# Blank rows of a sorted-token buffer written in an earlier stage, and one operand of a sum moved to TensorE

## The chip, the cores and the metric

One core of one Trainium2 chip runs the whole program. The metric is the device time of one execution in microseconds (us), the median of several runs. The core has TensorE (PE, with its weight loads as PEld), VectorE (DVE), ScalarE (ACT), GpSimd (POOL) and SyncE (SP), each with its own list of instructions; semaphores hold them together. The 16 DMA engines move data between HBM and the on-chip memory (SBUF).

## The reference

The input is x of 4 x 1024 tokens with 128 channels, float32. Four layers follow one another, each closed by a layer norm of x plus what the layer computes. Cut to what matters:

```python
x = _layernorm(x + _L0_attn_ref(x, ...))   # attention over channels' heads: 32 heads of 1024 keys of 64
x = _layernorm(x + _L0_ffn_ref(x, ...))    # attention with 16 heads, then 8 experts, top 2
x = _layernorm(x + _L1_attn_ref(x, ...))   # convolution, a scan over time, a gate
x = _layernorm(x + _L1_ffn_ref(x, ...))    # 8 experts; of a token's top 2 the one with the higher number counts
```

In the third layer, with `out_ssm` the scan's output through two products and their biases:

```python
x_res = jax.nn.silu(out_ssm @ W2.T)
z = out_ssm * x_res
return out_ssm + z @ Wlast.T
```

so the next norm takes x + out_ssm + z @ Wlast.T. In the fourth layer each token goes through one expert only.

## The kernel before, in words

The stages follow one another with a barrier between them. A tensor of tokens lies in SBUF with channels on the 128 partitions and the 4096 tokens along a partition (`xT` and `y`, in turn input and output of a stage).

**First attention** (`first_attention_stage`, from 23 to 493 us of the span). 32 heads; a head has 8 groups of 128 keys. Per group TensorE makes scores in PSUM (L315), VectorE takes the negated maximum (L388), ScalarE the exponential (L376), GpSimd scales the values (L423), TensorE mixes (L325). Beside groups 0 and 2 TensorE projects the next head's keys and queries (L294, L301), and ScalarE copies them out behind groups 2 and 4. The keys are needed on both halves of the partitions: SyncE doubles them by two DMAs per head (`double`, L274), which wait for the copied keys; the scores of the next head wait for the doubled keys. Behind each of the first 13 doublings SyncE issues one load of constants for the next stage (`loads`, L282). From the 14th head on it does nothing but double. Before the first product TensorE waits for two memsets of VectorE (L391, L392).

**Merged stage** (`scan_stage`, from 1441 to 1570.6 us), the scan. Blocks k = 0 to 15 are (batch, half of 512 tokens, group of 128 hidden channels), four to a batch. TensorE makes raw steps (L1617) and inputs (L1623); ScalarE four functions, the positive part, a square and the decay; GpSimd two products per block (`ratio`, L1749 and L1755); VectorE five operations per block (`step_size`), ending in `delta` and `b_bar`. At the end of a batch VectorE runs two scans of 1024 elements (L1805). Then, two batches of turns later in each engine's hand-written order: TensorE's `outs` (L1631, L1634), ScalarE's `take_out` into `out` (L1712), TensorE's `residuals` (L1643), ScalarE's silu into `res` (L1721), VectorE's `gate` (L1813), TensorE's `lasts` (L1653), and VectorE's `finish` (L1819). In parallel GpSimd adds the stage's input x to `out` (`add_x`, L1762) into `x_out`, and `finish` adds `x_out` and the product of `lasts` into y. `outs` of the next batch's second half waits for `finish` of a half before it (they share three PSUM banks), and `lasts` of a batch stands in TensorE's order behind the first `outs` of the next one and ahead of the inputs of a block. A product of 128 x 512 in float32 is two matmul instructions.

**Placing stage** (`place_stage`, from 1570.9 to 1643.5 us). Tokens are turned so that they lie on partitions, routed, and written as records of 136 words (128 channels, weight, output row, zeros) to a buffer in HBM, `scratch`. It has a region of 4096 + 128 rows for each expert, and behind the regions room for 40 tiles. The number of an expert's tokens is known only at the end; a tile is 128 rows, and the rest of an expert's last tile must hold blank records, whose output row lies behind the real output. The order of work: per batch (4 of them, 8 tiles each) VectorE chooses, scales, weighs and puts some 35 small operations; then GpSimd scatters eight tiles, each by an indirect DMA (L2170), and waits. Behind the last batch VectorE copies the experts' end rows to `pad_at` (L2122) and makes the table of tiles (`table`, ending in `tile_base`). GpSimd prepares the blank tiles at the start (L2161, L2164). SyncE's list: load `order` and the experts' weights; write eight blank tiles behind the regions (L1956); wait for `pad_at`; for each expert load a row number to a register and write one blank tile there (L1960, L1961); wait for the table, load four numbers to registers (L1963); wait for the blanks and for the scatters; load the first four tiles of records (L1968). The barrier follows. In the last stage SyncE loads the other 36 tiles (L2233) and all engines work on sorted tiles.

## Time and profile before

| | us |
|---|---|
| median of 3 runs | 1748.15 |
| lowest and highest run | 1747.13, 1757.48 |
| the profiled execution, its own time | 1751.21 |
| its span, first to last instruction | 1749.1 |

Over the span TensorE was busy 1548.7 us, VectorE 1320.5, ScalarE 1289.0 and GpSimd 545.2; the mean granted clock of TensorE was 0.933. Busy time says only how full an engine was; what a stage costs is read from which engine or queue ends it. All times in the rows are microseconds from the start of the span. Where a row carries a count (x4), its length runs from the first start to the last end. PEclk is the granted clock, 1.00 for 2.4 GHz and 0.50 for 1.2. SPq is SyncE's queue; "idle before" stands in square brackets with what ended it.

### The profile page before, as it was taken

How to read it: one execution, taken by the hardware profiler on the slowest of the kernel's cores; microseconds unless marked ns; L12 is line 12 of the kernel's file. 1: busy time of each engine (PE TensorE's matmuls, PEld its weight loads, DVE VectorE, ACT ScalarE, POOL GpSimd, SP SyncE). 2: the span in 40 equal slices, each digit the busy share in tenths (PEclk: the TensorE clock that was granted, in tenths of full speed). 3: DMA queues.
4: the chain of work that ended last, by engine and by line, in shares of the span. 5: the costliest groups of instructions: out<-in, count | busy, mean ns of one | idle time of the engine just before them, and what ended most of it. 6: DMA issues, size and time to landing. Idle time of an engine off the chain costs nothing. (4 is left out here: it accounts for less than half of the span.)

```text
span 1749.1 us, 38791 instructions
## 1 busy us (share of the span) xinstructions
PE 1548.7 (89%) x13958; PEld 837.6 (48%) x13958; DVE 1320.5 (75%) x1886; ACT 1289.0 (74%) x2465; POOL 545.2 (31%) x758
## 2 busy tenths in 40 slices
PE   5999999999988999999999999998899956772297
PEld 4555555555543344343434434336677622222286
DVE  2777777777759999999999999935554458976275
ACT  2777777777754998899988998976788757843186
POOL 0222222222245110100111012106788805634366
PEclk8999999999996999999999999988999987886599
DMA  2121100000014010011001101004245200003220
GB/s 76 28 90 54 54 18 18 18 18 18 18 22 129 13 31 12 5 25 30 5 9 31 27 4 38 5 5 98 56 91 97 50 15 0 1 16 142 63 65 33
DMA packets 37596, 66.71 MB, mean 38 GB/s; under 512 B 9744, under 2 KB 17688, under 8 KB 36960
## 3 DMA queue, kind: packets, MB, share of 16 engines
q1 hardware_dynamic: 32096, 58.14, 13.4%
q0 software_dynamic: 5376, 6.96, 1.4%
q8 instruction: 73, 1.20, 0.3%
q14 instruction: 51, 0.42, 0.1%
HBM read 32.49 MB, written 6.09 MB: 22 GB/s over the span
## 5 line engine op out<-in xcount | busy, mean ns | idle before, releaser
L1001 ACT ACTIVATE m_probs<-m_ring 128x512 f32<-128x512 f32 x1024 | 542.8, 597 | 81.3 <-PE m_ring L917 65.2
L1080 DVE TENSOR_REDUCE m_half_max<-m_pairs 128x2 f32<-128x1024 f32 x512 | 587.6, 1212 | 10.9 <-PE m_pairs L900 10.3
L388 DVE TENSOR_REDUCE a_neg_max<-a_scores 128x1 f32<-128x1024 f32 x257 | 310.5, 1215 | 90.8 <-PE a_scores L315 90.6
L376 ACT ACTIVATE a_probs<-a_scores,a_neg_max 128x1024 f32<-128x1024 f32 x256 | 285.4, 1115 | 123.3 <-DVE a_neg_max L388 123.3
L932 PE MATMUL m_acc<-m_probs,m_v_aug 128*32 128x256 f32 (+1 forms) x4032 | 331.0, 401 | 0.0
L917 PE MATMUL m_ring<-m_q_max,m_k 32*128 32x512 f32 x1024 | 319.0, 502 | 4.0 <-DVE m_q_max L1094 2.9
L900 PE MATMUL m_pairs<-m_k,m_q 32*128 32x512 f32 x1024 | 263.4, 512 | 13.4 <-DVE m_half_max L1080 9.6
L315 PE MATMUL a_scores<-a_q,a_k_own 64*128 64x512 f32 x516 | 259.8, 620 | 6.5 <-ACT a_probs L376 5.6
L315 PE MATMUL a_scores<-a_q,a_k_other 64*128 64x512 f32 x516 | 258.3, 620 | 0.8 <-ACT a_probs L376 0.3
L917 PEld LDWEIGHTS m_ring<-m_q_max,m_k 32*128 32x128 f32 x1024 | 146.4, 184 | 219.5 <-ACT m_probs L1001 117.0
L423 POOL TENSOR_TENSOR a_scaled<-values,a_inv 128x128 f32<-128x128 f32 x256 | 102.5, 400 | 388.5 <-DVE a_inv L406 257.7
L1446 POOL TENSOR_TENSOR e_g_parts<-e_gated,e_g_parts 128x512 fp32r<-128x512 f32 x128 | 165.5, 1323 | 38.0 <-ACT e_g_parts L1371 36.4
L1405 DVE TENSOR_TENSOR e_gated<-e_up,e_gates 128x512 f32<-128x512 f32 x128 | 87.2, 689 | 87.0 <-ACT e_up L1364 78.1
L932 PEld LDWEIGHTS m_acc<-m_probs,m_v_aug 128*32 128x32 f32 x4032 | 80.6, 109 | 125.7 <-ACT m_probs L1001 77.2
L325 PE MATMUL a_mixed<-a_probs,a_scaled 128*32 128x128 f32 x4128 | 139.2, 276 | 0.0
L325 PEld LDWEIGHTS a_mixed<-a_probs,a_scaled 128*32 128x32 f32 x4128 | 104.9, 109 | 56.2 <-issue 30.3
L315 PEld LDWEIGHTS a_scores<-a_q,a_k_other 64*128 64x128 f32 x516 | 86.0, 186 | 65.5 <-issue 32.8
L900 PEld LDWEIGHTS m_pairs<-m_k,m_q 32*128 32x128 f32 x1024 | 97.2, 187 | 28.5 <-DVE m_half_max L1080 23.1
L1364 ACT ACTIVATE e_up<-e_up,e_b 128x512 f32<-128x512 f32 x128 | 84.4, 660 | 32.9 <-PE e_up L1321 32.8
L315 PEld LDWEIGHTS a_scores<-a_q,a_k_own 64*128 64x128 f32 x516 | 86.0, 187 | 33.2 <-issue 24.3
L1180 POOL CAST m_max_cols<-m_row_max 128x16 fp32r<-128x16 f32 x32 | 6.8, 213 | 281.5 <-DVE m_row_max L1086 280.9
L1371 ACT ACTIVATE e_g_parts<-e_gated 128x512 fp32r<-128x512 f32 x128 | 79.8, 625 | 7.7 <-DVE e_gated L1405 7.7
(285 smaller groups left out, 2149.3 us busy)
## 6 DMA issues: line engine op xcount, KB each, us to landing
e_gates<-sorted_results SPq DMA_DIRECT2D x64, 256.0 KB, 8.6
a_k_other<-a_k_own SPq DMA_DIRECT2D x66, 128.0 KB, 2.3
m_k<-m_k_init SPq DMA_DIRECT2D x8, 512.0 KB, 6.8
m_q<-xT SPq DMA_DIRECT2D x8, 512.0 KB, 7.2
f_records<-sorted_tokens SPq DMA_DIRECT2D x40, 68.0 KB, 1.8
e_w<-e_w_dram SPq DMA_DIRECT2D x1, 2064.0 KB, 7.5
xT<-x_t_dram SPq DMA_DIRECT2D x1, 2048.0 KB, 7.8
m_v_aug<-v_init_dram SPq DMA_DIRECT2D x1, 2048.0 KB
```

The lines of the kernel that those rows point to most:

```text
L315: last = nc.tensor.matmul(scores[:, slot(i), h * BANK:(h + 1) * BANK], keys[rows, p, g // 2, :], q[rows, p, :, :].rearrange("p g t -> p (g ...
L325: last = nc.tensor.matmul(mixed[32 * j:32 * j + 32, :], scaled[:, g, j, 32 * e:32 * e + 32], probs[:, g, (2 * j + e) * TILE:(2 * j + e + 1 ...
L376: nc.scalar.activation(probs[:, g, :], scores[:, slot(h * G + g), :], ACT.Exp, bias=neg_max[:, g:g + 1], accum_out=total[:, g:g + 1]).then ...
L388: nc.vector.tensor_reduce(neg_max[:, i % G:i % G + 1], scores[:, slot(i), :], AX, ALU.max, negate=True).then_inc(max_done, 1)
L423: nc.gpsimd.tensor_tensor(scaled[:, g, :, :].rearrange("p j (e c) -> p j e c", c=48)[:, :, :, 0:16], values[:, ds(b * G, G), 16 * g:16 * g ...
L900: last = nc.tensor.matmul(pairs[:, pair % 2, m, :], q[batch % 2][rows, g, at:at + TILE], k[batch % 2][rows, g, a * BANK:(a + 1) * BANK], s ...
L917: nc.tensor.matmul(o, k[batch % 2][rows, n % GROUPS, u * TILE:(u + 1) * TILE], q_max[rows, number % 2, :], start=True, stop=True).then_inc ...
L932: last = nc.tensor.matmul(acc[32 * j:32 * j + 32, of], v_aug[:, g, u, j, :], probs[:, u % SLOTS, j, of], start=(g == 0 and u == 0), stop=( ...
L1001: nc.scalar.activation(probs[:, u % SLOTS, head, :], ring[:, bank, :], ACT.Exp, scale=0.5).then_inc(ring_taken, 1)
L1080: nc.vector.tensor_reduce(half_max[:, pair // PAIRS % 2, at:at + 2], pairs[:, pair % 2, :, :], AX, ALU.max).then_inc(pair_taken, 1)
L1405: nc.vector.tensor_tensor(gated[:, n % R, :], up[:, n % R, :], gates[:, c % 2, e, :], ALU.mult).then_inc(gated_done, 1)
L1446: nc.gpsimd.tensor_tensor(g_parts[:, 1, n % R, :], gated[:, n % R, :], g_parts[:, 0, n % R, :].bitcast(F32), ALU.subtract).then_inc(lo_don ...
```

## The change

Two edits. In the first, nothing depends any longer on where an expert's tokens end: each region is filled whole with blank records, before any token is scattered, in the first attention. SyncE does that in the 18 heads in which it had no load to issue, a small load of the rows' last 8 words (`rows_of`) in one head and the fill (`fill`) in the next; the fill's source is one tile of 8 records per partition, read four times over. The tile is made zero by GpSimd ahead of its loop. The placing stage loses the blank tiles, `pad_at` and the waits for them.

```diff
-def first_attention_stage(core, xT, y, w_q, w_k, values, loads):
+def first_attention_stage(core, xT, y, w_q, w_k, values, loads, scratch, blank_rows):
...
+        blank = core.sb("a_blank", [D, BLANK_ROWS, RECORD], F32, st)
...
+                def rows_of(e):
+
+                    sp.wait_ge(blank_zero, 1)
+                    if e:
+                        sp.wait_ge(filled, 32 * e)
+                    sp.dma_start(blank[:, :, D:].bitcast(U32), blank_rows[:, e, :, :]).then_inc(blank_rows_in, 16)
+
+                def fill(e):
+
+                    sp.wait_ge(blank_rows_in, 16 * (e + 1))
+                    all_rows = blank[:, :, :].rearrange("p j d -> p (j d)")
+                    at = e * REGION
+                    if e == E:
+                        at += (SORT_TILES - UNUSED) * TILE
+                        sp.dma_start(scratch[at:at + UNUSED * TILE, :].rearrange("(p j) d -> p (j d)", j=BLANK_ROWS),
+                                     all_rows).then_inc(filled, 16)
+                        return
+                    wide = [D, N // (D * BLANK_ROWS), BLANK_ROWS * RECORD]
+                    sp.dma_start(scratch[at:at + N, :].rearrange("(c p j) d -> p c (j d)", p=D, j=BLANK_ROWS),
+                                 all_rows.unsqueeze(1).broadcast_to(wide)).then_inc(filled, 16)
+                    sp.dma_start(scratch[at + N:at + REGION, :].rearrange("(p j) d -> p (j d)", j=BLANK_ROWS),
+                                 all_rows[0:TILE // BLANK_ROWS, :]).then_inc(filled, 16)
...
                 for head in range(TILES):
...
                         sp.dma_start(to, at).then_inc(loaded, 16)
+                    else:
+                        e, at = divmod(head - len(loads), 2)
+                        if e <= E:
+                            if at == 0:
+                                rows_of(e)
+                            else:
+                                fill(e)
+                sp.wait_ge(filled, 16 * (2 * E + 1))
                 sp.wait_ge(keys_doubled, DUP * (TILES + 1))
...
             @block.gpsimd
             def _(pool):
+                nc.gpsimd.memset(blank[:, :, :], 0.0).then_inc(blank_zero, 1)
                 pool.wait_ge(zeroed, 1)
...
                 for to, at in loads[1:]:
                     sp.dma_start(to, at).then_inc(loaded, 16)
-                sp.wait_ge(blank_set, 1)
-                last = E * REGION + (SORT_TILES - UNUSED) * TILE
-                sp.dma_start(scratch[last:last + UNUSED * TILE, :].rearrange("(t p) d -> p t d", p=TILE),
-                             blank[:, E:, :]).then_inc(padded_done, 16)
-                sp.wait_ge(pads_known, 1)
-                for e in range(E):
-                    at = sp.value_load(pad_at[0:1, e:e + 1], min_val=0, max_val=E * REGION)
-                    sp.dma_start(scratch[ds(at, TILE), :], blank[:, e, :]).then_inc(padded_done, 16)
                 sp.wait_ge(table_made, 1)
...
-                sp.wait_ge(padded_done, 16 * (E + 1))
                 sp.wait_ge(scattered, 16 * TILES)
...
-                    then(nc.vector.tensor_copy(pad_at[0:1, :], start[0:1, :]))
-                    dve.sem_inc(pads_known, 1)
...
-                nc.gpsimd.memset(blank[:, :, :], 0.0).then_inc(blank_zero, 1)
-                pool.wait_ge(blank_zero, 1)
-                pool.wait_ge(order_in, 16)
-                nc.gpsimd.tensor_copy(blank[:, :, D + 1].bitcast(U32), rows_of_out[:, TILES:]).then_inc(blank_set, 1)
```

The second edit is in the merged stage. TensorE puts x into the PSUM bank by a product with the identity, ahead of `lasts`' own product, which now adds to it; `finish` adds `out` in place of `x_out`.

```diff
                 def lasts(b):
                     for h in range(2):
-                        pe.wait_ge(gated_done, 2 * b + h + 1)
                         if h == 0:
                             pe.wait_ge(out_done, 2 * b + 2)
                         else:
                             pe.wait_ge(res_done, 2 * b + 1)
-                        nc.tensor.matmul(bank(b, 2, h), w[:, WLAST_AT, :], gated[:, h, :], start=True,
+                        nc.tensor.matmul(bank(b, 2, h), ident, x[:, half_of(b, h)], start=True, stop=False)
+                        pe.wait_ge(gated_done, 2 * b + h + 1)
+                        nc.tensor.matmul(bank(b, 2, h), w[:, WLAST_AT, :], gated[:, h, :], start=False,
                                          stop=True).then_inc(last_ready, 1)
...
-                def add_x(b):
-                    for h in range(2):
-                        pool.wait_ge(out_done, 2 * b + h + 1)
-                        if b:
-                            pool.wait_ge(y_done, 2 * (b - 1) + h + 1)
-                        nc.gpsimd.tensor_tensor(x_out[:, h, :], x[:, half_of(b, h)], out[:, b % 2, part(h)],
-                                                ALU.add).then_inc(x_out_done, 1)
-
-                for k in range(TURNS):
-                    if k < K:
-                        ratio(k)
-                    if k % BLOCKS_OF == 2 and k >= 2 * BLOCKS_OF:
-                        add_x(k // BLOCKS_OF - 2)
+                for k in range(K):
+                    ratio(k)
...
                     dve.wait_ge(last_ready, 2 * b + h + 1)
-                    dve.wait_ge(x_out_done, 2 * b + h + 1)
-                    nc.vector.tensor_tensor(y[:, half_of(b, h)], x_out[:, h, :], bank(b, 2, h), ALU.add).then_inc(y_done, 1)
+                    nc.vector.tensor_tensor(y[:, half_of(b, h)], out[:, b % 2, part(h)], bank(b, 2, h),
+                                            ALU.add).then_inc(y_done, 1)
```

## Rows read from the trace of the kernel before

**Rows 1.** Busy time by engine in three stretches (table of windows)

```profile
core 0: us, PE busy (x) PEld busy (x) DVE busy (x) ACT busy (x) POOL busy (x), PEclk, DMA share, GB/s
30.00:390.00 360.00, 353.50 (x4384) 200.39 (x4385) 262.77 (x424) 259.38 (x451) 79.26 (x198) 0.99 0.14 37
...
1500.00:1550.00 50.00, 33.72 (x59) 13.00 (x58) 48.12 (x46) 33.53 (x50) 29.02 (x16) 0.78 0.00 0
...
1600.00:1650.00 50.00, 3.34 (x12) 2.57 (x12) 17.19 (x70) 4.39 (x15) 22.88 (x26) 0.50 0.18 53
```

**Rows 2.** Order of time, end of the placing stage: start, length, engine, line, idle before

```profile
1612.18 0.95 POOL L2170 DMA_INDIRECT sorted_tokens<-p_records,p_slots  x1 [5.40 <-DVE p_slots L2116]
...
1622.11 16.48 SPq L1961 DMA_DIRECT2D sorted_tokens<-p_blank  x8
...
1624.69 0.19 DVE L2044 TENSOR_TENSOR tile_base<-p_base,e_order 1x42 int32<-1x42 f32 x1
...
1631.14 0.96 POOL L2170 DMA_INDIRECT sorted_tokens<-p_records,p_slots  x1 [0.30 <-issue]
...
1641.52 1.95 SPq L1968 DMA_DIRECT2D f_records<-sorted_tokens  x4
```

**Rows 3.** Order of time of SyncE's queue, and the landings of the record loads

```profile
1624.94 0.70 SPq L1961 DMA_DIRECT2D sorted_tokens<-p_blank  x1
...
1629.19 0.71 SPq L1961 DMA_DIRECT2D sorted_tokens<-p_blank  x1
...
1637.15 0.33 SPq L1961 DMA_DIRECT2D sorted_tokens<-p_blank  x1
...
1638.25 0.34 SPq L1961 DMA_DIRECT2D sorted_tokens<-p_blank  x1
...
DMA to landing us min/median/max: 1.7/1.8/2.5
```

**Rows 4.** Order of time: VectorE in the placing stage's third batch

```profile
1608.11 0.20 DVE L2088 RECIPROCAL p_inv<-p_total 128x8 f32<-128x8 f32 x1 [4.05 <-issue]
```

**Rows 5.** First attention: SyncE's and TensorE's order, and two windows' DMA rates

```profile
99.12 1.10 SPq L274 DMA_DIRECT2D a_k_other<-a_k_own  x2
...
113.01 1.10 SPq L274 DMA_DIRECT2D a_k_other<-a_k_own  x2
...
310.76 1.10 SPq L274 DMA_DIRECT2D a_k_other<-a_k_own  x2
...
318.34 0.69 PE L315 MATMUL a_scores<-a_q,a_k_other 64*128 64x512 f32 x1
...
102.00:104.00 2.00, 2.00 (x39) 1.33 (x40) 0.74 (x2) 2.00 (x5) 0.53 (x2) 1.00 0.93 393
...
1586.00:1588.00 2.00, 0.85 (x4) 0.52 (x3) 1.65 (x10) 0.26 (x1) 1.07 (x1) 0.72 0.46 110
```

**Rows 6.** Order of time: VectorE, then GpSimd, merged stage; then GpSimd, placing stage

```profile
1504.17 3.37 DVE L1813 TENSOR_TENSOR d_gated<-d_out,d_res 128x512 f32<-128x512 f32 x2
...
1546.24 1.75 DVE L1778 SCALAR_TENSOR_TENSOR d_front<-d_squared,d_z 128x512 f32<-128x512 f32 x1
...
1556.23 1.26 DVE L1813 TENSOR_TENSOR d_gated<-d_out,d_res 128x512 f32<-128x512 f32 x2
...
1502.07 4.93 POOL L1762 TENSOR_TENSOR d_x_out<-y,d_out 128x512 f32<-128x512 f32 x2
...
1561.76 1.27 POOL L1762 TENSOR_TENSOR d_x_out<-y,d_out 128x512 f32<-128x512 f32 x1 [7.61 <-DVE xT L1819]
...
1570.92 1.91 POOL L2161 MEMSET p_blank<- 128x2176 f32 x1 [4.34 <-POOLq L1610]
```

**Rows 7.** Order of time, merged stage: a row of VectorE, two of TensorE

```profile
1518.34 1.02 DVE L1778 SCALAR_TENSOR_TENSOR d_front<-d_squared,d_z 128x512 f32<-128x512 f32 x1 [0.67 <-ACT d_squared L1699]
...
1559.87 1.88 PE L1653 MATMUL d_out_ps<-d_gated,s_w 128*128 128x512 f32 x4
...
1567.93 1.98 PE L1653 MATMUL d_out_ps<-d_gated,s_w 128*128 128x512 f32 x4 [1.51 <-DVE d_gated L1813]
```

More of the change, by code:

```diff
@@ L26 @@
 E = 8
+SORT_TILES = (N + E * (TILE - 1)) // TILE + 1
+SORT_TILES += -SORT_TILES % 4
+TABLE = SORT_TILES + 2
+REGION = N + TILE
+UNUSED = 8
+RECORD = D + 8
+DUMP = E + UNUSED
+BLANK_ROWS = 8
+U32 = mybir.dt.uint32
+I32 = mybir.dt.int32
 class Core:
@@ L253, in first_attention_stage @@
         loaded = core.sem("a_loaded")
+        blank = core.sb("a_blank", [D, BLANK_ROWS, RECORD], F32, st)
+        blank_zero = core.sem("a_blank_zero")
+        blank_rows_in = core.sem("a_blank_rows_in")
+        filled = core.sem("a_filled")
         CREDIT = G
@@ L1529, with scan_stage @@
 LOG_SLOPE, LOG_BASE = 2.535488718105198, 2.734703737275435
-def scan_stage(core, x, xa, w, vecs, y):
+def scan_stage(core, x, xa, w, vecs, ident, y):
     nc = core.nc
@@ L1555, in scan_stage @@
         quad, front, log1p, delta = (ring(n, s) for n, s in (("quad", 2), ("front", 2), ("log1p", 2), ("delta", 4)))
-        res, gated, x_out = ring("res", 2), ring("gated", 2), ring("x_out", 2)
+        res, gated = ring("res", 2), ring("gated", 2)
         a_bar, b_bar, state = (core.sb(f"d_{n}", [D, 2, 2, S], F32, st) for n in ("a_bar", "b_bar", "state"))
@@ L1585, in scan_stage @@
         last_ready = core.sem("d_last_ready")
-        x_out_done = core.sem("d_x_out_done")
         y_done = core.sem("d_y_done")
@@ L1836, in _ @@
                         gate(b)
-SORT_TILES = (N + E * (TILE - 1)) // TILE + 1
-SORT_TILES += -SORT_TILES % 4
-TABLE = SORT_TILES + 2
 PER = BANK // D
-REGION = N + TILE
-UNUSED = 8
-RECORD = D + 8
-DUMP = E + UNUSED
-U32 = mybir.dt.uint32
-I32 = mybir.dt.int32
 def place_stage(core, src, mean_w, ident, router, order, records, scratch, tile_expert, tile_base, loads, sorted_records,
@@ L1871, in place_stage @@
     at = D + E * (PER_BATCH + 1)
-    tile_rows, rows_of_out = order[:, at:at + TABLE], order[:, at + TABLE:at + TABLE + TILES + DUMP]
-    at += TABLE + TILES + DUMP
+    tile_rows, rows_of_out = order[:, at:at + TABLE], order[:, at + TABLE:at + TABLE + TILES]
+    at += TABLE + TILES
     region, earlier_first = order[:, at:at + E], order[:, at + E:at + 2 * E]
@@ L1881, in place_stage @@
         eps = core.sb("p_eps", [D, 1], F32, st)
-        blank = core.sb("p_blank", [TILE, DUMP, RECORD], F32, st)
-        pad_at = core.sb("p_pad_at", [1, E], I32, st)
         turned = core.ps("p_turned", [TILE, 2, BANKS, BANK], st)
@@ L1924, in place_stage @@
         recorded = core.sem("p_recorded")
-        blank_zero = core.sem("p_blank_zero")
-        blank_set = core.sem("p_blank_set")
-        pads_known = core.sem("p_pads_known")
         table_made = core.sem("p_table_made")
-        padded_done = core.sem("p_padded_done")
         scattered = core.sem("p_scattered")
@@ L2149, in _ @@
                 dve.wait_ge(order_in, 16)
-                nc.vector.tensor_copy(records[:, :, D + 1].bitcast(U32), rows_of_out[:, 0:TILES]).then_inc(recorded, 1)
+                nc.vector.tensor_copy(records[:, :, D + 1].bitcast(U32), rows_of_out).then_inc(recorded, 1)
                 then(nc.vector.tensor_copy(counts[:, :, 0], region))
@@ L2472, in build @@
                     constants.append((tiles.q[0][:, g, :].bitcast(F32), xT[:, PAD + N:PAD + N + S]))
-                first_attention_stage(core, xT, y, w_q, w_k, values, constants)
+                first_attention_stage(core, xT, y, w_q, w_k, values, constants, scratch, a["blank_rows"])
             tiles.add(core, st)
@@ L2496, in build @@
             convolution_stage(core, tokens_y, w, vecs, xa)
-            scan_stage(core, tokens_y, xa, w, vecs, tokens_x)
+            scan_stage(core, tokens_y, xa, w, vecs, ident, tokens_x)
         with ExitStack() as st:
@@ L2588, in layouts @@
         np.broadcast_to(np.arange(TABLE) * TILE, (D, TABLE)),
-        row[:, None] + TILE * np.arange(TILES + DUMP),
+        row[:, None] + TILE * np.arange(TILES),
         np.broadcast_to(np.arange(E) * REGION, (D, E)),
         np.broadcast_to(np.arange(E, 0, -1) / 16, (D, E))], axis=1).astype(np.float32)
+    behind_end = N + (row[:, None] * BLANK_ROWS + np.arange(BLANK_ROWS))
+    blank_rows = np.zeros((D, E + 1, BLANK_ROWS, RECORD - D), np.uint32)
+    for e in range(E):
+        blank_rows[:, e, :, 1] = N + TILE * e + (behind_end - N) % TILE
+    blank_rows[:, E, :, 1] = behind_end + TILE * E
     def of_channels(v):
@@ L2609, in layouts @@
         "s_w": np.ascontiguousarray(s_w.transpose(2, 0, 1)),
+        "blank_rows": blank_rows,
         "s_vecs": np.ascontiguousarray(s_vecs),
```

## The prediction

> **What bounds the kernel now.** I read the table of stages first, to see which engine is full in each stage that the change touches; then the order of time at their joints; then single rows for durations. In the first attention [rows 1] TensorE is busy 353.50 of 360 us, and DMA takes 0.14 of its engines' time: the first attention ends when TensorE ends. In the merged stage (the scan) VectorE is busy 48.12 of 50 us and TensorE 33.72: VectorE sets the time, until its last scan is over; from there TensorE, ScalarE and VectorE follow each other one by one. From 1600 to 1650 no engine is busy half the time. There the order of time counts [rows 2]: GpSimd issues its 16 last scatters back to back from 1612.18 to 1632.10, VectorE has the table ready at 1624.88, SyncE writes the eight blank tiles from 1622.11 to 1638.59, and its first load of sorted records leaves only at 1641.52; the next stage opens some 2 us behind it, once all four are issued. Everything waits for SyncE's own list of instructions, 9.4 us after the last scatter was issued.
>
> **Part 1, the pads leave the placing stage.** One blank tile costs SyncE a register load, a few register operations and a DMA. Undisturbed the tiles leave every 1.09 us (from 1637.15 to 1638.25), but while GpSimd scatters they are over 4 us apart: 1624.94, then 1629.19 [rows 3]. Behind the last one come four register loads for the table: 1641.52 - 1638.59 = 2.9 us. After the change SyncE has nothing to do but wait for the table (1624.88), and it makes the four loads while GpSimd still issues: even at the slow turn's 4.25 us for each, two are done by 1633.4 and the other two, undisturbed, by 1634.5. Then it waits for the scatters. The last was issued at 1631.14 for 0.96 us [rows 2]; its own landing isn't shown; the only landings shown nearby, of the record loads, take 1.7 to 2.5 us [rows 3]. I put its landing at 1632.10 + 2.2 = 1634.3, and the first record load there in place of 1641.52: 7.2 us gained, of which I take 7.1. The Trainium skill (DMA: Bandwidth & Descriptors, Anatomy of one DMA) puts a fixed cost near 2.0 us on a GpSimd-issued DMA, most of it the receipt of the write; no row here shows that landing, and by the page it would be 1634.1.
>
> GpSimd's memset and cast of the blanks end at 1573.55, far ahead of its first scatter, and are worth 0. VectorE's copy of the start rows is one of some 14 small operations ahead of the table (0.2 us with its wait), which no longer ends last: 0. The 544 KB write beside the expert weights goes too; nothing waits for those weights before 1645: 0.
>
> What could move is the start of the scatters. VectorE stood still for 4.05 us in the third batch with nothing to wait for [rows 4], and GpSimd's last 16 scatters begin only when that batch's slots are there (1612.18), though it was free 5.4 us earlier. If such a standstill doesn't come back, 5 us more are gained; if it comes into the last batch, some are lost. I take 0 and keep 5 us to both sides.
>
> **Part 2, the regions are filled in the first attention.** Per expert: one load of 1024 little pieces and one fill of 2.23 + 0.07 = 2.30 MB, on SyncE's queue, in turns of two heads. Eight fills, then 0.56 MB. All DMAs of this queue share their engines with the doubling of the keys, so that is what can be late. Its doubling at 310.76 is followed by the next head's first scores at 318.34 [rows 5]; issue 1.10 and landing 2.3 end near 313.6, which leaves 4.7 us. The fill is issued at 311.9; the next doubling comes 13.9 us after the last, at 324.65. A fill may thus take 12.7 + 4.7 = 17.4 us before TensorE stops for a key. Behind the doubling of 99.12 SyncE issues a load of 2.0 MB; it moved 393 GB/s at its height, and the next doubling came at 113.01, 13.89 us later as everywhere: TensorE didn't feel it [rows 5]. At that rate a fill takes 6 to 8 us. The slow end is the tail of the blanks' own write to HBM in 544-byte pieces, 110 GB/s with DMA engines busy 0.46 of the time: 21 us, 4 to 5 us late, times 8 = about 40 us. The fill's pieces are 4352 bytes long (eight records), nearer to the first row; I take 0 and keep 40. The pieces of the little load have 13 us to themselves. The last, small fill is issued near 467 and the stage's work ends near 493, so the new wait at SyncE's end is over; only the end of the stage is queued behind it.
>
> GpSimd's new memset (half of the one that took 1.91 us) runs while VectorE makes the two memsets for which TensorE waits. The two could hold each other up for its whole length, 1.0 us, or not at all [rows 6]; neither reads SBUF, and the only stretched pairs in the trace do: I take 0.
>
> **Part 3, the merged stage.** GpSimd loses eight additions. Alone one takes 1.27 us; two beside a scan and the gates took 4.93, and the gates took 3.37 in place of 1.26 [rows 6]. That happens in batches 0 and 1: 2 x 2.1 = 4.2 us off the engine that sets the time. In batch 2 the addition lies beside an operation that took 1.75 for 0.69: 1.06 us. Step operations that then slip out of the shadow of GpSimd's other products may give up to 1.7 us, others slip into it; I take 0.5. Sum 5.8. The sum to y has the same shape as before: 0.
>
> The Trainium skill (SBUF — State Buffer, SBUF: two separate sides) calls the port pair that VectorE and GpSimd share an exclusive lock for a whole instruction. The gates' row fits a lock. By the rule each addition that came before a VectorE operation would give back its full 1.27 us, five of them 6.3 us in place of my 5.3 from rows; the time would be 1 us lower, 1737.4.
>
> TensorE gets eight products, two instructions each. At the high clock one is 1.88 / 4 = 0.47, steady 0.43 us [rows 7], so 0.86 per half. Three places count. (a) Batch 0: the four extra instructions stand ahead of the product for the next step sizes; ScalarE starts on those at once after its last work and would wait 1.3 us; VectorE has 0.67 us of wait in this loop already [rows 7]: loss 0.6. In batch 1 TensorE idles 4 us behind the same place: 0. (b) Batch 2, behind the last scan: the last products of batch 2 at 1559.87 [rows 7] and then the first ones of batch 3, which ScalarE awaits, follow each other without a gap: 2 x 0.86 = 1.7. (c) Batch 3: the identity for half 0 fits in ahead of the gate, while ScalarE makes the silu, but the one for half 1 stands between the last products of 1567.93: 0.86. Sum 3.2. If all sixteen ran at the low clock and all were on the path it would be 16 x 0.85 = 13.6; below 0.86 it can't be, as (c) has no cover. Net of this stage: 5.8 - 3.2 = 2.6 gained.
>
> **Sum.** 7.1 + 2.6 = 9.7 us. The profiled execution took 1751.2 (its span of 1749.1 and 2.1 around it), so it would take 1741.5. It lay 3.1 above the median of the runs, 1748.15; the same gain gives 1738.4. A measurement tells about 1% (17 us) from no change.
>
> **The rivals.** (R1) SyncE's slow stretch beside the scatters isn't the rule in ordinary runs. At 1.09 us a tile the blanks are out by 1621 + 8 x 1.09 = 1630, the table loads by 1633, and the scatters' landing at 1634.3 was already last: only the merged stage gains, 1745.5. For it: two tiles later the pace is 1.09. Against: the standstills must be in the ordinary time too, since profiled and median differ by 3 us only. (R2) TensorE's additions bind wherever they stand, at the low clock: 13.6 - 5.8 = 7.8 lost, 7.1 gained: 1748.9. For: VectorE waits for TensorE's products at both ends of a batch; against: 16 us of idle TensorE in these 50. (R3, the other side) The fills hold back the doubling of the keys. From 143 GB/s downward (2.30 MB in 16 us) each fill stops TensorE; at 110 GB/s it is 5 us, eight times: 1738.4 + 40 = 1778. For: it is the one rate to HBM in the trace, and the engines were half idle at it; against: the pieces are eight times as long. (R4) The standstills of VectorE in the placing stage go with the pads: 1733.
>
> **How the numbers follow.** Forecast 1738.4: 0.53. R1 0.16, R2 0.09, R3 0.05, R4 0.12, and 0.05 for other losses. The range goes from R4 with 2 us more to R1 and the edge of R2: 1731 to 1748. Faster by over 1% (under 1730.7) needs R4 and a lucky merged stage: 0.06. Slower by over 1% is R3 and part of the rest: 0.06. Within 1%: 0.88.
>
> **What would show it.** In the profile after: doublings of the keys still 13.89 us apart, also behind a fill, and fills that land in under 12 us; gates of 0.65 us each in all four batches; the first record load some 2.2 us behind the last scatter, and SyncE in a wait before it; the last sums to y about 1.7 + 0.9 us later behind the last scan than now. It is wrong if TensorE waits for a doubled key, if the merged stage (from 1441 to 1570.9 now) isn't 1 to 4 us shorter, or if the first record load stays over 5 us behind the last scatter.

## The result, and the profile after

The changed kernel takes 1734.83 us in the median of 11 runs (1730.46 to 1741.85); the kernel before took 1747.13 (11 runs, the three shown among them). The ratio is 0.9926, 95% interval [0.9908, 0.9944]: 9.8 to 16.1 us less. A ratio here and below isn't the quotient of the two medians (that would be 0.9930 here; in experiment 1 it would be 0.9965 for 0.9950), and it leaves out two runs that took over twice as long as all others, which the medians count (3788.75 us in experiment 3, 4775.40 us of the kernel before beside experiments 1 to 4). The forecast was 1738.4, 9.7 less. The profiled execution took 1741.85 (span 1740.0), 9.4 less than the profiled one before.

A table of the stages from the two traces shows where the 9.1 us of the span went (start of a stage's first instruction to that of the next):

```
                                     before   after
up to the norm                       1397.7  1398.7   +1.0
norm and convolution                   43.4    46.0   +2.6
merged stage                          129.9   124.6   -5.3
placing stage                          73.0    66.4   -6.6
last stage                            105.2   104.4   -0.7
```

The two stages in question give 11.9 us, and the last one 0.7. What lies ahead of them gave 3.6 back in this pair of executions. That is scatter: the norm and the convolution, which no kernel here changes, were between 42.8 and 46.3 us long in the profiles of the experiments.

**The stretches of [rows 1].** Table of windows of the kernel after, the columns as there:

```profile
core 0: us, PE busy (x) PEld busy (x) DVE busy (x) ACT busy (x) POOL busy (x), PEclk, DMA share, GB/s
30.00:390.00 360.00, 353.67 (x4384) 200.77 (x4385) 262.48 (x423) 258.95 (x449) 78.93 (x198) 0.99 0.24 75
1444.60:1569.20 124.60, 88.46 (x160) 33.15 (x160) 101.49 (x107) 90.80 (x136) 50.98 (x32) 0.86 0.00 0
...
243.00:248.00 5.00, 5.00 (x81) 2.97 (x80) 3.56 (x5) 3.77 (x7) 1.19 (x3) 1.00 1.02 411
```

In the first attention DMA's share rose from 0.14 to 0.24, and TensorE is as busy as before. The last row is a fill at work: 411 GB/s, so 2.30 MB in 5.6 us. SyncE's order around that fill answers to [rows 5]:

```profile
240.61 1.10 SPq L291 DMA_DIRECT2D a_k_other<-a_k_own  x2
241.76 0.59 SPq L312 DMA_DIRECT2D sorted_tokens<-a_blank  x1
242.39 0.55 SPq L314 DMA_DIRECT2D sorted_tokens<-a_blank  x1
254.50 1.11 SPq L291 DMA_DIRECT2D a_k_other<-a_k_own  x2
```

The doubling behind the fill comes 254.50 - 240.61 = 13.89 us after the one ahead of it, as without a fill. (The prediction's "as everywhere" isn't quite so: every fourth distance is 14.99 us, before and after.)

**The end of the placing stage** answers to [rows 2] (order of time):

```profile
1610.93 0.96 POOL L2178 DMA_INDIRECT sorted_tokens<-p_records,p_slots  x1 [5.53 <-DVE p_slots L2130]
...
1623.37 0.19 DVE L2058 TENSOR_TENSOR tile_base<-p_base,e_order 1x42 int32<-1x42 f32 x1
...
1630.24 0.95 POOL L2178 DMA_INDIRECT sorted_tokens<-p_records,p_slots  x1 [0.30 <-issue]
1632.71 2.30 SPq L1982 DMA_DIRECT2D f_records<-sorted_tokens  x4
```

The first record load comes 1632.71 - 1631.19 = 1.5 us behind the issue of the last scatter; before it was 9.4. What SyncE waits for now, from the table of its waits in 1600 to 1645:

```profile
SPq L1982 <- DMA sorted_tokens<-p_records,p_slots: 5.2, 1, 5.2
```

The standstill of VectorE in the third batch [rows 4] is still there:

```profile
1606.67 0.20 DVE L2102 RECIPROCAL p_inv<-p_total 128x8 f32<-128x8 f32 x1 [3.31 <-issue]
```

**The merged stage** answers to [rows 6] and [rows 7]. Order of time of VectorE: the gates and two step operations of batch 0, the gates of batch 1, and the last scan with the gates of batch 2:

```profile
1506.45 1.26 DVE L1851 TENSOR_TENSOR d_gated<-d_out,d_res 128x512 f32<-128x512 f32 x2
...
1509.02 1.57 DVE L1820 SCALAR_TENSOR_TENSOR d_log1p<-d_quad,d_front 128x512 f32<-128x512 f32 x1
1510.62 1.41 DVE L1826 TENSOR_TENSOR d_delta<-d_positive,d_log1p 128x512 f32<-128x512 f32 x1
...
1533.12 2.06 DVE L1851 TENSOR_TENSOR d_gated<-d_out,d_res 128x512 f32<-128x512 f32 x2
...
1544.94 0.68 DVE L1816 SCALAR_TENSOR_TENSOR d_front<-d_squared,d_z 128x512 f32<-128x512 f32 x1
...
1548.44 4.47 DVE L1843 TENSOR_TENSOR_SCAN d_state<-d_a_bar,d_b_bar 128x1024 f32<-128x1024 f32 x2
1552.82 1.27 DVE L1851 TENSOR_TENSOR d_gated<-d_out,d_res 128x512 f32<-128x512 f32 x2
```

The gates of batch 0 went from 3.37 to 1.26 and the front of batch 2 from 1.75 to 0.68. In batch 1 the first gate is still long (2.06 for the two). The last scan takes 4.47 where it took 5.49. But log1p and delta, 0.69 each when nothing runs beside them, are now 1.57 and 1.41: GpSimd's own products have moved ahead and lie beside them. TensorE behind the last scan (it ends at 1552.91):

```profile
1553.14 1.12 PE L1679 MATMUL d_out_ps<-s_xa,s_w 128*128 128x512 f32 x2 [1.21 <-ACT d_res L1770]
1554.10 1.88 PE L1682 MATMUL d_out_ps<-d_state,s_w 128*128 128x512 f32 x4
1555.82 1.02 PE L1700 MATMUL d_out_ps<-y,consts_sb 128*128 128x512 f32 x2
1556.67 1.02 PE L1702 MATMUL d_out_ps<-d_gated,s_w 128*128 128x512 f32 x2
1557.53 1.02 PE L1700 MATMUL d_out_ps<-y,consts_sb 128*128 128x512 f32 x2
...
1565.40 1.13 PE L1702 MATMUL d_out_ps<-d_gated,s_w 128*128 128x512 f32 x2 [0.65 <-DVE d_gated L1851]
1566.36 1.02 PE L1700 MATMUL d_out_ps<-y,consts_sb 128*128 128x512 f32 x2
1567.22 1.02 PE L1702 MATMUL d_out_ps<-d_gated,s_w 128*128 128x512 f32 x2
```

Line 1700 is the identity: two ahead of the gates' products of batch 2, and the one at 1566.36 between the last two products. The first row is new too: the product that opens batch 3's sums waits for ScalarE's silu of batch 2 (`res`) and starts only 0.2 us behind the end of the last scan, where before it was done 1.5 us ahead of it.

### The profile page after: what moved, and what is told of

It reads as the page before. It is cut to its first block and busy times, and to the rows that moved or that the text cites. A ratio compares the mean times of both kernels' runs of the same rounds, so it can differ in the third digit from the quotient of the medians.

```text
span 1740.0 us, 38771 instructions
## 1 busy us (share of the span) xinstructions
PE 1553.6 (89%) x13974; PEld 841.7 (48%) x13974; DVE 1314.6 (76%) x1885; ACT 1289.3 (74%) x2465; POOL 528.1 (30%) x749
## 5 line engine op out<-in xcount | busy, mean ns | idle before, releaser
L424 ACT ACTIVATE a_probs<-a_scores,a_neg_max 128x1024 f32<-128x1024 f32 x256 | 285.4, 1115 | 123.3 <-DVE a_neg_max L436 123.3
```

Of the source, the lines that this page charges most:

```text
L424: nc.scalar.activation(probs[:, g, :], scores[:, slot(h * G + g), :], ACT.Exp, bias=neg_max[:, g:g + 1], accum_out=total[:, g:g + 1]).then ...
```

## The experiments

Every run left a profile that can be read for the same stages. Experiments 1 to 4 ran on one chip, 5 to 8 on a second and 9 to 12 on a third, each with its own runs of the kernel before; a ratio is always against those. (Of the pair above the chip isn't known.) "The loop" is the merged stage up to the end of its last scan, "the tail" what follows to the last sum.

**1. The first edit alone.** The kernel after with the merged stage of before.

> Only the pads move (fills in the first attention, none in the placing stage); the merged stage is the one of before. Forecast's theory: 7.1 us less than before (ratio 0.9959), the first record load 1.5 to 2.3 us behind the last scatter in place of 9.4. Profile after showed the placing stage 6.6 shorter. Rival R1 (SyncE's slow stretch is a thing of the profile): 0 to 2 us less (ratio 0.999 to 1.000). Rival R4 (standstills of VectorE go too): 12 us less, and no standstill of 3 us or more in the third batch.

Measured: 1738.65 against 1744.73, ratio 0.9950 [0.9923, 0.9977], 4.0 to 13.4 us less. The first record load comes 1.5 us behind the last scatter; VectorE's standstill is 2.61 us. On this chip both R1 and R4 are out: the gain is there in ordinary runs, and the standstill is too. SyncE's first record loads (the last scatter's issue ended at 1630.54):

```profile
1632.06 2.40 SPq L1993 DMA_DIRECT2D f_records<-sorted_tokens  x4
```

**2. The second edit alone.** The kernel before with the merged stage of after.

> Only the merged stage changes (identity products in place of GpSimd's additions); pads as before. Forecast's theory: 2.6 us less than before (ratio 0.9985). By the profile after, where this stage was 5.3 shorter: 5 to 6 less (0.9970). Rival R2 (TensorE's additions bind): 8 us more (1.0045).

Measured: 1744.37 against 1744.73, ratio 0.9988 [0.9966, 1.0009]: between 5.9 less and 1.6 more. The time alone settles nothing; the trace says more. The loop took 107.7 us (before: 115.3), the tail 16.06 (before: 14.33).

**3. Nobody adds x.** The second edit without its identity products:

```diff
-                        nc.tensor.matmul(bank(b, 2, h), ident, x[:, half_of(b, h)], start=True, stop=False)
...
-                        nc.tensor.matmul(bank(b, 2, h), w[:, WLAST_AT, :], gated[:, h, :], start=False,
+                        nc.tensor.matmul(bank(b, 2, h), w[:, WLAST_AT, :], gated[:, h, :], start=True,
```

> As the kernel before, but nobody adds the input x in the merged stage (left out of the result): neither GpSimd nor TensorE. It separates what GpSimd's additions cost from what TensorE's products cost. Theory of the forecast: 5.8 us less than before, so 3.2 less than with the identity products. If the products cost nothing and the whole 5.3 is what the additions had cost, it equals the run with the identity products. Rival on the clock (the identity products keep TensorE's clock up behind the last scan, where the three products of C took 1.88 for four instead of 3.68): here the low clock is back behind the last scan, those four take 3.68 again, and this run is no faster, or even slower, than the one with the identity products.

Measured: 1739.23, ratio 0.9944 [0.9913, 0.9974]. The loop took 108.4 us, no less than with the products; the tail 13.59, so the identity products cost 16.06 - 13.59 = 2.5 us, all of it behind the last scan, and nothing ahead of it. The clock rival fell: without the identity products TensorE ran at the full clock there as well (order of time of TensorE, the last scan ending at 1552.30):

```profile
1552.38 1.12 PE L1630 MATMUL d_out_ps<-s_xa,s_w 128*128 128x512 f32 x2 [1.27 <-ACT d_res L1720]
1553.34 1.88 PE L1633 MATMUL d_out_ps<-d_state,s_w 128*128 128x512 f32 x4
1555.06 1.88 PE L1652 MATMUL d_out_ps<-d_gated,s_w 128*128 128x512 f32 x4
```

In the profile before, the four products of C (the ones with `d_state`, the first to need the last scan) took 3.68 us:

```profile
1556.36 3.68 PE L1634 MATMUL d_out_ps<-d_state,s_w 128*128 128x512 f32 x4 [1.56 <-DVE d_state L1805]
```

That was a thing of that one execution. Three later profiles with the old merged stage (experiments 1, 5 and 6) show 1.98 there, at a granted clock of 1.00 (2.4 GHz), where the profile before had 0.51 to 0.55 (1.2 GHz). TensorE had idled 1.56 us ahead of them in that profile, and 0.97 to 1.11 us in the three. Such a row, of the one with the pads kept:

```profile
1559.87 1.98 PE L1683 MATMUL d_out_ps<-d_state,s_w 128*128 128x512 f32 x4 [0.97 <-DVE d_state L1854]
```

So the old form's tail is 12.65 us rather than 14.3 when the clock is up, and the change's tail of 16.05 costs 3.4 us, not 1.7. The products are 2.5 of that. The other 0.9 is the first row of the three above. The silu that it waits for stands at the end of a chain: a sum of VectorE (`finish`), TensorE's products of C for the other half of batch 2, ScalarE's `take_out` and silu. From that `finish` to the end of the last scan VectorE now needs 9.16 us instead of 11.26; the chain still needs 9.2 to 9.4 to the opening product, and so ends last. Behind the last scan the products of C start 1.04 us late (1.19 with the identity products) where it was 0.06. That the chain is so long is TensorE's clock in it: the four products of C took 3.62 us in the kernel after, at a granted clock of 0.50, and 2.55 in experiment 11, at 0.74, where the products behind the scan are only 0.13 late. First the kernel after, then experiment 11:

```profile
1546.34 3.62 PE L1682 MATMUL d_out_ps<-d_state,s_w 128*128 128x512 f32 x4
```

```profile
1540.29 2.55 PE L1683 MATMUL d_out_ps<-d_state,s_w 128*128 128x512 f32 x4
```

Over the ten profiles of the new form it is so throughout: where the four took 3.47 to 3.62 us (eight), the wait is 1.0 to 1.2 us; where they took 2.6 (experiments 4 and 11), it is 0.14 at most.

**4. The identity twice.** Experiment 2 with a second identity product behind the first.

> As the run with only the merged stage changed, but every identity product is made twice (the input is added twice in the result). Forecast's theory: another 3.2 us (0.86 in each of some four uncovered places) lost against the single one. If only the last half's is uncovered: 0.4 to 0.9 us lost.

Measured: 1744.82, ratio 0.9997 [0.9974, 1.0021], which can't be told from experiment 2. In the trace the tail is 17.60, 1.5 us more than with one. Three second products are 3 x 0.86 = 2.6, and 1.05 of it is hidden: the wait for the silu is 0.14 here and was 1.19 in experiment 2. The loop is 110.4, 2.7 more. VectorE's wait for ScalarE in batch 0, 0.67 before [rows 7], is 1.7 us here (table of VectorE's waits, 1504.46 to 1562.46):

```profile
DVE xT L1808 <- PE d_out_ps L1654: 4.3, 2, 3.5
DVE d_front L1768 <- ACT d_squared L1700: 1.7, 1, 1.7
```

So place (a) of the prediction exists. With one identity product it was 0.9 in the kernel after and nothing in experiment 2: one product is nearly covered, the second isn't.

**5. The fills alone.** The kernel before with the fills added and nothing taken away.

> The kernel before with the fills added in the first attention and nothing taken away: the pads are still written in the placing stage, over the same rows. It prices the fills alone. Forecast's theory: 0 (ratio 1.000, within 0.2%), doublings of the keys 13.89 us apart, placing stage 73 us as before. Rival R3 (a fill holds back the doubling): up to 40 us more (1.023). The profile after already showed 13.89.

Measured: 1746.35 against 1744.72, ratio 0.9993 [0.9965, 1.0022]. The doublings are as far apart as before; the placing stage is 70.9 us. The fills cost nothing that 0.3% would show.

**6. The pads at fixed rows.** As experiment 5, with

```diff
-                    at = sp.value_load(pad_at[0:1, e:e + 1], min_val=0, max_val=E * REGION)
-                    sp.dma_start(scratch[ds(at, TILE), :], blank[:, e, :]).then_inc(padded_done, 16)
+                    at = e * REGION + N
+                    sp.dma_start(scratch[at:at + TILE, :], blank[:, e, :]).then_inc(padded_done, 16)
```

> As the run with fills and pads both, but SyncE writes the eight pads to fixed rows (the last tile of each region), so it makes no register load for them and needn't wait for the start rows; the eight DMAs stay. Forecast's theory (SyncE's register loads are what crawls beside GpSimd's scatters): the pads leave about 1 us apart or less, the first record load comes 1.5 to 2.5 us behind the last scatter, the placing stage is 6 to 7 us shorter than with the pads at loaded rows (66 to 67 us). Rival (the DMAs' issue itself crawls beside the scatters, 4 us a tile): the stage stays near 72 us or gains 2 to 3 us at most.

Measured: 1738.48, ratio 0.9961 [0.9933, 0.9988]. SyncE's queue, first with the rows loaded (experiment 5), then fixed:

```profile
1623.42 15.36 SPq L2001 DMA_DIRECT2D sorted_tokens<-p_blank  x8
1641.25 1.94 SPq L2008 DMA_DIRECT2D f_records<-sorted_tokens  x4
```

```profile
1612.25 3.69 SPq L2001 DMA_DIRECT2D sorted_tokens<-p_blank  x8
1625.88 2.11 SPq L2008 DMA_DIRECT2D f_records<-sorted_tokens  x4
```

Eight DMAs in the midst of the scatters (1604.10 to 1624.00) take 3.69 us, 0.46 each. The same eight with a register load ahead of each take 15.36. (The loop still waited for the start rows; that wait had stayed.) The record loads come 1.9 us behind the last scatter, and the placing stage is 65.5 us, as short as in the kernel after (66.4) and in experiment 1 (65.5). So eight DMAs by themselves aren't slow between scatters; the list is slow in the form that has a register load and operations on registers ahead of each. Which part of it is hit isn't separated. The loop has 48 instructions there, experiment 6 has 8, and in the slow stretch of the kernel before every kind is held now and then: the issue of a DMA (0.70 us in [rows 3]) and even the assertion on the loaded row (duration in ns as min/median/max):

```profile
L1960 SPq SEQ_ASSERT  x8: 1/18/690, 1621.1 to 1638.0; - x8
```

**7. Three fills a turn**, the second and third into rows that nobody reads.

> As the kernel after, but each region is filled three times (twice into rows that nobody reads), so 6.8 MB a turn instead of 2.3. The profile after showed 2.30 MB in 5.6 us at 410 GB/s. Forecast's theory (a turn may take 17.4 us of DMA before TensorE waits for a doubled key): three fills take 17 to 18 us, the doubling behind them lands up to 1 us late: 0 to 8 us more over eight turns. If the slack is smaller than read: each us less costs 8 us. If anything else in the first attention hangs on the queue, more.

Measured: 1736.70, ratio 0.9954 [0.9926, 0.9983]. The order of SyncE's queue around the last turns:

```profile
384.87 1.10 SPq L291 DMA_DIRECT2D a_k_other<-a_k_own  x2
386.01 1.18 SPq L314 DMA_DIRECT2D sorted_tokens<-a_blank  x2
387.24 1.27 SPq L316 DMA_DIRECT2D sorted_tokens<-a_blank  x1
388.55 2.32 SPq L318 DMA_DIRECT2D sorted_tokens<-a_blank  x1
398.76 1.90 SPq L291 DMA_DIRECT2D a_k_other<-a_k_own  x2
```

At 406 GB/s the three last 16.7 us, and the doubling at 398.76 takes 1.90 us to issue instead of 1.10. Each of its DMAs lands 6.9 us behind its issue instead of 2.4, so 4.5 late. The next doubling is late by 0.9, 0.7, 0.8 and 0.7 us behind the second, fourth, sixth and eighth fill; behind the other four, where the next doubling is due after 14.99 us, nothing is lost. The stage is 474.5 us long, 4.1 more than with one fill: 3.1 of it are these four turns, and 1.0 arises in the first two heads, ahead of any fill. A doubling that lands 4.5 late and costs 0.7 to 0.9 had 3.8 us to spare, where the prediction read 4.7; its bound of 17.4 us is 12.7 + 3.8 = 16.5.

**8. Scatters held.**

```diff
-                    pool.wait_ge(slots_done, b + 1)
+                    pool.wait_ge(slots_done, B)
```

> As the kernel after, but GpSimd holds all its scatters until the slots of the last batch are there, so nothing is scattered beside VectorE's and ScalarE's four batches. The stage gets longer by some 20 us, since 32 scatters of 1.26 us then stand behind the batches. What counts is the standstill of VectorE in the third batch (4.05 us before, 3.31 after, 2.6 to 3.8 in the runs so far) and of ScalarE beside it (4.3 to 8.3 us). Theory: they come from the scatters; both are gone, and the table is ready 2.5 to 4 us earlier behind the stage's start. Rival (they come from something else, such as code that has to be fetched): they are there as before.

Measured: 1761.28 us, in one run. The placing stage is 87.4 us, 21 longer than in the kernel after. The same instruction of VectorE as in [rows 4]:

```profile
1606.97 0.20 DVE L2102 RECIPROCAL p_inv<-p_total 128x8 f32<-128x8 f32 x1
```

No idle time before it, and the table is ready 46.3 us behind VectorE's first instruction of the stage, against 54.3 in the kernel after. The theory holds, and its size was too small: GpSimd's scatters cost VectorE and ScalarE 8 us in this stage, only 3.3 of them in the standstill that stands out.

**9. A second fill in pieces of 544 bytes.**

> As the kernel after, with each region filled a second time (into rows that nobody reads) in pieces of 544 bytes, one record each, 2.23 MB a turn. It measures the slow end on which rival R3 stood: 110 GB/s for such pieces, at which the second fill alone would take 20 us, the doublings behind it come late, and TensorE waits some 8 to 10 us in each of eight turns (1.8% in all). If small pieces move at 200 GB/s or more, the second fill takes 11 us or less, both fills stay within 17.4 us, and no doubling is late.

Measured: 1725.72 us in one run (the kernel before took 1732.2 on this chip). No doubling is late: the distances are those of before. The window in which the small pieces move:

```profile
300.00:307.00 7.00, 7.00 (x114) 3.89 (x108) 5.21 (x9) 5.24 (x10) 1.60 (x4) 1.00 1.16 294
```

Pieces of 544 bytes move at 294 GB/s with the DMA engines full; both fills together take 7.6 + 5.6 = 13.2 us, within the slack of 16.5. The 110 GB/s on which R3 stood [rows 5] was a DMA that didn't fill the engines (0.46 busy). By these rates R3 could not have come about at either size of piece.

**10 to 12. Third chip: the identities first, both ways, and the kernel after again.** In experiment 10 `lasts` makes both identity products ahead of its waits for the gates. In experiment 11 batches 0 and 1 take the identity, batches 2 and 3 GpSimd's addition:

```diff
+                        if b < 2:
+                            nc.tensor.matmul(bank(b, 2, h), ident, x[:, half_of(b, h)], start=True, stop=False)
...
+                for b in (2, 3):
+                    for h in range(2):
+                        pool.wait_ge(out_done, 2 * b + h + 1)
+                        if b == 2 and h == 0:
+                            pool.wait_ge(gated_done, 2 * b + 2)
+                        if b == 3:
+                            pool.wait_ge(y_done, 2 * (b - 1) + h + 1)
+                        nc.gpsimd.tensor_tensor(x_out[:, h, :], x[:, half_of(b, h)], out[:, b % 2, part(h)],
+                                                ALU.add).then_inc(x_out_done, 1)
```

> As the kernel after, but both identity products of a batch stand ahead of the waits for its gates, so that in batch 3 no product but the last one stands behind the second gate. Theory (term c: 0.86 us on the path in batch 3; term b, batch 2, is not touched, as its gates are long done): from the last scan to the last sum 15.2 us in place of 16.05, under 0.1% in time. If the products hide behind something else there: 16.05 as before.

> As the kernel after, but only batches 0 and 1 take the identity products; in batches 2 and 3 GpSimd adds the input as before, and in batch 2 only once VectorE has made its gates. Theory: the additions cost time only beside VectorE's scans and steps, the identity products only behind the last scan, so this has the gain of one without the cost of the other: the loop as long as after's (108.3 us to the end of the last scan), from there 13.6 us in place of 16.05, as in the run without x; 2 to 2.5 us less than after (0.9987). If GpSimd's two additions hold up what stands beside them in the tail: 0 to 1 us less.

> The kernel after, unchanged, on the same chip as the two runs that alter its merged stage, so that they can be set against it. Expected: 0.9926 of before, with a merged stage of 124.6 us and a placing stage of 66.4.

Measured, before taking 1732.20: experiment 10 1727.41, ratio 0.9974 [0.9956, 0.9992]; experiment 11 1725.72, 0.9961 [0.9942, 0.9980]; the kernel after 1726.86, 0.9956 [0.9934, 0.9977]. The three can't be told apart. In the traces the tail is 15.5 us in experiment 10 (0.5 less than 16.05, where 0.86 was expected) and 12.7 in experiment 11 (13.6 expected). But experiment 11's loop took 110.3 us instead of 108.3; 1.7 of it is there by batch 0's first sum, up to which its code is that of the kernel after. And its tail owes 0.9 of its 12.7 us to TensorE's clock in the chain to the silu (experiment 3): 13.6 - 0.9 = 12.7, so GpSimd's additions cost the tail nothing. Stage by stage experiment 11 is 1.3 us shorter than the kernel after on the same chip (123.3 against 124.6); as a time of the whole kernel that isn't shown.

This chip holds the largest surprise. The kernel after, unchanged, has a placing stage of 60.9 us on it (66.4 in the first profile). GpSimd never waits for slots between its 32 scatters, and the same instruction of VectorE has no standstill, with scatters beside it:

```profile
1603.71 0.96 POOL L2178 DMA_INDIRECT sorted_tokens<-p_records,p_slots  x1 [0.30 <-issue]
1603.83 0.20 DVE L2102 RECIPROCAL p_inv<-p_total 128x8 f32<-128x8 f32 x1
```

SyncE's four register loads of the table (instructions of one source line: count, durations in ns as min/median/max, first and last start), in the first profile after and then on this chip, both beside scatters:

```profile
L1978 SPq FUSED_REGOPS  x4: 3/167/700, 1624.2 to 1626.5; - x4
```

```profile
L1978 SPq FUSED_REGOPS  x4: 147/150/187, 1611.6 to 1613.3; - x4
```

All four profiles on this chip are free of the standstill. All nine of the other kernels that scatter beside the batches, the two profiles of before and after among them, have it, with 2.6 to 4.05 us. Whether it is the chip or something else of that session the runs don't tell.

## Why the prediction held, point by point

The time lies in the range, 3.6 us below the forecast, and the forecast's gain of 9.7 is just outside the measured interval of 9.8 to 16.1. By the time alone rival R4 (1733) is nearer than the forecast; what rules it out on these chips is the profile, where the standstill is still there. By the stages, over all profiles:

- **What bounds the kernel.** Right at all three places. SyncE's list set the end of the placing stage: four later kernels with loaded pads have the first record load 7.7 to 8.3 us behind the last scatter, the kernels without 1.5.
- **Part 1, the landing.** Put at 2.2 us behind the issue, measured 1.5 in the kernel after and within 0.1 us of it in seven more; the 1.5 even holds SyncE's own first operations for the record load. The size failed by where it was counted from: the landings of [rows 3] run from the start of an issue, and the forecast added them to the end of one that takes 0.96 us. Experiment 12's profile has landings of scatters, 2.3 us (median) from the start of the issue and so some 1.35 from its end. The Trainium skill (DMA: Bandwidth & Descriptors, Anatomy of one DMA) has 2.0 for the fixed part; that is near the rows if it is counted from the start of the issue, and too much if it is added to its end. The gain at this joint was put at 7.1 and is 7.9 in the pair of profiles, but 6.8 in the mean (8.3 - 1.5): the profile before had the longest stretch of all.
- **Part 1, the start of the scatters.** 0 with 5 to both sides: the placing stage as a whole gained 6.6 in the pair and 5.6 in the mean of the profiles that aren't from the third chip (71.7 with loaded pads in five kernels, 66.1 in three without). The 5 us kept for a vanishing standstill exist; they come on the third chip, or with the scatters held, and not with the pads (R4).
- **Why SyncE crawled.** The prediction said the tiles were slow beside scatters, without naming the part. DMAs alone aren't (experiment 6); the list with register loads is, whether by the loads or by the number of its instructions. The forecast that the table's four loads would be done before the scatters' end held: they took 3.6 us beside scatters, from 1623.64 to 1627.23.
- **Part 2.** 0, and measured 0 (experiment 5); the slack of 17.4 us was right to a microsecond (16.5, experiment 7); the slow end of 110 GB/s was no end (experiment 9). R3's own sum didn't fit the slack: it put the limit at 16 us (143 GB/s), and by the 17.4 the fills at 110 GB/s would have been 3.5 us late, 28 in all and not 40. GpSimd's memset took 1.00 us at 23.14 and VectorE's two beside it are as long as before.
- **Part 3, the gains.** Gates 4.2: in the kernel after 2.11 + 1.32 = 3.4 (the sign of 0.65 us each failed in batch 1, where GpSimd's own product lies beside the first gate), in experiment 2 all of the 4.2. Front 1.06: measured 1.07. The step that failed in size is the 0.5 us for operations that slip out of the shadow of GpSimd's products: the whole loop gained 6.7 us (115.0 in the mean of four profiles of the old form, 108.3 of seven of the new), so this rest is near 2; 1.0 of it is the last scan (5.49 to 4.47), which I had not counted as touched. The Trainium skill's exclusive lock (SBUF — State Buffer, SBUF: two separate sides) would have had 6.3 in place of 5.3 for these additions, which is nearer to the loop's 6.7. The rows fit that rule. Of GpSimd's two products

```profile
1508.40 1.63 POOL L1798 TENSOR_TENSOR d_z<-d_u,d_inverse 128x512 f32<-128x512 f32 x1 [4.02 <-ACT d_inverse L1735]
1510.11 1.37 POOL L1804 TENSOR_TENSOR d_q<-d_z 128x512 f32<-128x512 f32 x1
```

the first ends at 1510.03; the log1p that began at 1509.02 would end 0.69 behind it, at 1510.72, and ended at 1510.59; the delta would end at 1511.48 + 0.69 = 1512.17, and ended at 1512.03. Each is held until GpSimd's instruction is over, to within 0.15 us.
- **Part 3, the losses.** (b) and (c) together 2.56: measured 2.5 (experiment 3). (a) 0.6: VectorE's wait there is 0.93 in the kernel after and none in experiment 2, where it was 0.67, so at most 0.3 with one product, and it is real with two (experiment 4). Put at nothing without a word: 0.9 us because ScalarE's silu of batch 2 is late once VectorE is faster and TensorE's clock is low ahead of it. That is the new wait of this stage. Net 6.7 - 3.4 = 3.3 in the mean of the profiles, where 2.6 was put; the 5.3 of the first pair holds 1.7 us of low clock in the profile before. By the prediction's own sign (1 to 4 us shorter) the pair would have refuted this part; only the mean is inside. The last sums came 1.7 us later behind the last scan in the pair and 3.4 against the three other profiles of the old form, where 2.6 was put.
- **Sum.** 5.6 + 3.3 = 8.9 us by the profiles' means, 9.7 by the forecast, 12.3 by the medians. The 3.4 us between the first and the last aren't found in any stage; differences of that size lie between runs of one kernel. The two single edits measured 8.7 and 2.1 less (experiments 1 and 2, 0.9950 and 0.9988, each with half-widths of 4 to 5 us), which add up to that within their intervals. The result is within 1%, the case that had 0.88.
- **The rivals.** R1 was named for "ordinary runs" and lives on another condition: on the third chip SyncE doesn't crawl. There the first edit should have gained little, and the whole kernel's ratio is 0.9956, 4.0 to 11.4 us less. No profile of the kernel before was taken on that chip, so how much of this is the first edit stays open. R2 and R3 are out.

## What to carry to other kernels

Where an engine's instruction list ends last, look for what makes it slow and not only for how much it has to do: a DMA to a fixed address cost 0.46 us beside GpSimd's scatters, a register load with its DMA up to 4.2, on chips where the scatters slow anything. An addition that is free on an idle engine is not free beside VectorE, and one moved to TensorE is free only while VectorE is at work: count it in the loop and behind the loop apart, and ask which engine is next once the first one is faster. Before a row of one profile carries a term, see whether its clock is the usual one.

## What the hardware showed that I had not expected

- Beside back-to-back indirect DMAs of GpSimd, the other engines' instructions were held in steps of 0.70 us in nine profiles (in the one before, three of VectorE's start at 1608.11, 1608.82 and 1609.52): 8 us of the 54 that VectorE needs for its table in the placing stage, up to 4.2 us for one register load and DMA of SyncE. Scatters alone don't set it: set against experiment 12, VectorE of the kernel before loses its 8 us between 27 and 39 us of the stage and nothing in the 15 us behind, with scatters beside it in both. On a third chip nothing of it was to be seen with the same program.
- The same code behind the last scan ran at 0.51 to 0.55 of the full clock in one profile and at 1.00 in three, for 1.7 us. In the second attention, which no kernel changes, the clock differs too: from its first product to its end it took 660 us in four profiles with a mean granted clock of 0.968, 666 to 667 in five with 0.956, 668 to 669 in four with 0.952 and 669.3 in one with 0.949. Runs of one kernel differ by 10 to 20 us, and 9 of it can come from here. A part of the stage in two profiles of one chip (the kernel after, then experiment 11):

```profile
1100.00:1190.00 90.00, 80.46 (x710) 33.40 (x707) 51.80 (x67) 65.77 (x126) 10.49 (x15) 0.85 0.01 3
```

```profile
1100.00:1190.00 90.00, 80.63 (x733) 36.79 (x731) 54.16 (x70) 70.70 (x135) 10.77 (x16) 0.92 0.05 11
```
